# Attention with a fourth score bank, one shared output bank, and transposes four units behind the scores

## What is computed

```python
# layer 1: 16 heads of 32 channels, 512 queries and 512 context tokens, 4 batches
q = _w8a8_linear(x, wq, bq)        # 8-bit activations and weights
k = cond @ wk.T + bk
v = cond @ wv.T + bv
scores = einsum('bhnd,bhld->bhnl', q, k) / sqrt(32) + mask
attn = softmax(scores, axis=-1)
o = einsum('bhnl,bhld->bhnd', attn, v)
x = x + tanh(g) * _w8a8_linear(o, wo, bo)
# then the feed-forward of the layer, with rounded weights and activations
```

## Time and profile before

| | us | share |
|---|---|---|
| median of three runs | 1017.13 | |
| the profiled execution's own time | 1016.46 | |
| its span in the profile | 1014.7 | |
| TensorE matmuls busy | 899.2 | 89% |
| TensorE weight loads busy | 587.9 | 58% |
| VectorE busy | 673.4 | 66% |
| ScalarE busy | 573.6 | 57% |
| exponentials, line 1322, 256 of them | 175.0 | |
| masks, line 1732, 256 of them | 174.0 | |
| granted TensorE clock, mean | 0.969 of full speed | |

### The profile page before, as it was taken

One profiled execution on the slowest core, in us unless ns is written; L12 is line 12 of the kernel. 1 busy time (PEld: TensorE's weight loads), 2 busy tenths in 40 slices (PEclk: granted clock), 3 DMA queues, 4 the chain that ended last, 5 costly groups with the idle time before them and its releaser, 6 DMA issues.

```text
span 1014.7 us, 15824 instructions
## 1 busy us (share of the span) xinstructions
PE 899.2 (89%) x5592; PEld 587.9 (58%) x5592; DVE 673.4 (66%) x1870; ACT 573.6 (57%) x1094; POOL 86.9 (9%) x105
## 2 busy tenths in 40 slices
PE   3989998999999787899999999999999899999467
PEld 2868765676767453666444666445666444666233
DVE  5895860524250073798777898777798776799564
ACT  4545233355553132788347788357788447789153
POOL 2000213021120005100100000100000100000100
PEclk9999999999999999799999999999999999999769
DMA  6444556452450059510199110198110188100001
GB/s 195 141 142 159 196 205 228 146 164 86 135 198 1 23 164 197 115 43 2 42 182 191 43 43 2 42 180 186 51 43 1 43 175 196 46 2 1 1 1 42
DMA packets 52270, 102.82 MB, mean 101 GB/s; under 512 B 8924, under 2 KB 8924, under 8 KB 50656
## 3 DMA queue, kind: packets, MB, share of 16 engines
q1 hardware_dynamic: 39872, 71.88, 27.1%
q10 hardware_dynamic: 8160, 17.31, 5.1%
q0 software_dynamic: 4160, 12.62, 4.0%
HBM read 55.62 MB, written 14.75 MB: 69 GB/s over the span
## 4 chain that ended last, share of the span: by engine, by line
PE 36%; DVE 9%; issue 6%; ACT 5%; SPq 4%; DMA 3%; POOL 1%; POOLq 0%; DVEq 0%; ACTq 0%
PE psum L1494 7%; PE psum L1462 6%; PE psum L1567 5%; PE psum L1511 5%; PE psum L1537 5%; SPq L1185 4%; ACT probs L1322 3%; DMA k<-k_lo 3%; PE psum L1429 1%; PE psum L1553 1%; PE psum L1520 1%; DVE amax L1670 1%; DVE xn L1842 1%; DVE stats L1837 1%; DVE xn L1658 1%
## 5 line engine op out<-in xcount | busy, mean ns | idle before, releaser
L1322 ACT ACTIVATE probs<-psum,neg_max 128x512 f32<-128x512 f32 x256 | 175.0, 692 | 46.5 <-DVE neg_max L1732 46.5
L1732 DVE CUSTOM_DVE_ANT_0 psum<-psum,m_in 128x512 f32<-128x512 f32 x256 | 174.0, 703 | 18.3 <-issue 18.3
L1494 PE MATMUL psum<-ident,probs 128*128 128x128 f32 x1024 | 154.2, 275 | 0.0
L1494 PEld LDWEIGHTS psum<-ident,probs 128*128 128x128 f32 x1024 | 127.8, 141 | 19.8 <-issue 2.6
L1462 PE MATMUL psum<-k,q 128*128 128x512 f32 x256 | 125.7, 496 | 15.3 <-ACT probs L1322 6.8
L674 PE MATMUL psum<-w_sb,hT 128*128 128x512 f32 x256 | 117.6, 604 | 5.6 <-ACT hT L566 5.6
L1762 DVE COPY probsT<-psum 128x512 f32<-128x512 f32 x128 | 87.8, 686 | 2.7 <-PE psum L1494 2.5
L1313 ACT COPY probsT<-psum 128x512 f32<-128x512 f32 x128 | 75.3, 588 | 20.3 <-PE psum L1494 20.3
L594 PE MATMUL psum<-xselT_hi,w_hi 128*128 128x256 f32 x256 | 81.8, 320 | 1.6 <-ACT xselT_hi L501 1.6
L674 PEld LDWEIGHTS psum<-w_sb,hT 128*128 128x128 f32 x256 | 47.0, 192 | 55.3 <-issue 48.5
L1462 PEld LDWEIGHTS psum<-k,q 128*128 128x128 f32 x256 | 49.1, 192 | 51.7 <-ACT probs L1322 31.5
(11 more groups left out here) (221 smaller groups left out, 1566.7 us busy)
## 6 DMA issues: line engine op xcount, KB each, us to landing
bw_raw<-in_L_ffn_W_dram ACTq DMA_DIRECT2D x16, 1024.0 KB, 5.3
c_in<-in_ctx_dram SPq DMA_DIRECT2D x8, 1024.0 KB, 5.5
k<-k_hi SPq DMA_DIRECT2D x24, 256.0 KB, 5.9
k<-k_lo SPq DMA_DIRECT2D x24, 256.0 KB, 6.7
q<-q_hi SPq DMA_DIRECT2D x48, 128.0 KB, 3.9
q<-q_lo SPq DMA_DIRECT2D x48, 128.0 KB, 3.4
xres<-in_x_dram SPq DMA_DIRECT2D x4, 1024.0 KB, 5.9
w_raw<-in_L_ffn_w_dram POOLq DMA_DIRECT2D x4, 1024.0 KB, 5.4
```

The costliest lines, as they stand in the source:

```text
L1322: act.activation(probs[:, u % 4, :], psum[u % SCORE_BANKS][:, :], ACT.Exp, scale=-1.0, bias=neg_max[:, u:u + 1], accum_out=prob_sum[:, nt, ...
L1494: mm = pe.transpose(turn_bank(u)[:, l * P:(l + 1) * P], probs[:, u % 4, l * P:(l + 1) * P], ident[:, :])
L1732: dve.tensor_tensor_reduce(bank[:, :], bank[:, :], m_in[:, nt, :], -1.0, LOWEST, ALU.add, ALU.min, neg_max[:, u:u + 1]).then_inc(masked_re ...
```

## The change

Banks 0 to 3 hold scores, 4 to 6 turned units, and bank 7 (`OUT_BANK`) alone takes the value sum and the turned output of every half group. The transposes of a unit stand four steps behind its score, and four first scores and masks are issued ahead. The two value groups of a half group stand two steps apart. `attnT` is copied by ScalarE in the step between them (its wait spans the second group), its transposes follow three steps after the second group, and the division one step later. The first value group of a half group now waits for the division of the one just before. The context copies of ScalarE move from step 68 to step 70, which puts them behind the last `attnT` copy. The wait and the memset ahead of each mask are taken out.

```diff
-        LAG = 3
+        LAG = 4
-        SCORE_BANKS, TURN_BANKS = 3, 3
+        SCORE_BANKS, TURN_BANKS = 4, 3
-        AV_STEPS = 4
-        STEPS = UNITS + LAG + UH + 3
-        CONTEXT_BANKS = (0, 1, 2, 4)
+        AV_STEPS = 2
+        STEPS = UNITS + LAG + UH - 1
+        OUT_BANK = 7
+        CONTEXT_BANKS = (0, 1, 2, 3)
...
# ScalarE
-                        if more and s == UNITS + LAG + 1:
+                        if more and s == UNITS + LAG + 2:
                             turned_context(b + 1)
...
-                        hg = past_half_group(s, 1)
+                        hg = past_half_group(s, -6)
                         if hg is not None:
                             act.wait_ge(av_psum, b * HG + hg + 1)
-                            act.copy(attnT[:, hg % 2, :], psum[6 + hg % 2][:, 0:HALF]).then_inc(av_ready, 1)
+                            act.copy(attnT[:, hg % 2, :], psum[OUT_BANK][:, 0:HALF]).then_inc(av_ready, 1)
...
# TensorE
+                            elif b and SCORE_BANKS + u == OUT_BANK - 1:
+                                pe.wait_ge(x_done, b * T)
...
-                        if 0 <= hg < HG and i % AV_STEPS == 0:
+                        if 0 <= hg < HG and i in (0, AV_STEPS):
...
-                                if hg >= 2:
-                                    pe.wait_ge(o_ready, b * HG + hg - 1)
+                                if hg:
+                                    pe.wait_ge(o_ready, b * HG + hg)
                                 else:
                                     pe.wait_ge(x_done, b * T + 1)
-                            for l in range(T * i // UH, T * (i + AV_STEPS) // UH):
+                            for l in range(T * i // (2 * AV_STEPS), T * (i + AV_STEPS) // (2 * AV_STEPS)):
...
-                        hg = past_half_group(s, 3)
+                        hg = past_half_group(s, -2)
                         if hg is not None:
                             pe.wait_ge(av_ready, b * HG + hg + 1)
...
# VectorE
-                    if u >= 4:
-                        dve.wait_ge(probs_ready, b * UNITS + u - 3)
-                    dve.memset(held[:, u % 4:u % 4 + 1], 0.0)
...
-                        hg = past_half_group(s, 2)
+                        hg = past_half_group(s, -2)
...
-                        hg = past_half_group(s, 3)
+                        hg = past_half_group(s, -1)
```

More of the change, by code:

```diff
@@ L1503, in attend @@
                                     context(b + 1, c_in)
-                                if hg >= 2:
-                                    pe.wait_ge(o_ready, b * HG + hg - 1)
+                                if hg:
+                                    pe.wait_ge(o_ready, b * HG + hg)
                                 else:
                                     pe.wait_ge(x_done, b * T + 1)
-                            for l in range(T * i // UH, T * (i + AV_STEPS) // UH):
+                            for l in range(T * i // (2 * AV_STEPS), T * (i + AV_STEPS) // (2 * AV_STEPS)):
                                 for r in range(HPG):
                                     h = (hg // 2) * HPG + r
-                                    mm = pe.matmul(psum[6 + hg % 2][HD * r:HD * (r + 1), 0:HALF],
+                                    mm = pe.matmul(psum[OUT_BANK][HD * r:HD * (r + 1), 0:HALF],
                                                    vv[:, l, h * HD:(h + 1) * HD],
@@ L1519, in attend @@
                             for k in range(2):
-                                mm = pe.transpose(psum[6 + hg % 2][:, HALF + k * P:HALF + (k + 1) * P],
+                                mm = pe.transpose(psum[OUT_BANK][:, HALF + k * P:HALF + (k + 1) * P],
                                                   attnT[:, hg % 2, k * P:(k + 1) * P], ident[:, :])
@@ L1777, in attend @@
                                 xn[:, n0:n0 + 2, g * P:(g + 1) * P].rearrange("p t (r d) -> p t r d", r=HPG),
-                                psum[6 + hg % 2][:, HALF:2 * HALF].rearrange("p (t r d) -> p t r d", t=2, r=HPG),
+                                psum[OUT_BANK][:, HALF:2 * HALF].rearrange("p (t r d) -> p t r d", t=2, r=HPG),
                                 prob_inv[:, n0:n0 + 2, g * HPG:(g + 1) * HPG].unsqueeze(3).broadcast_to([P, 2, HPG, HD]),
```

## The result

The changed kernel took 1030.0 us (median of 4, 1029.44 to 1031.15) against 1017.21 us before (median of 4, 1016.01 to 1017.87). The ratio is 1.0134, 95% interval 1.0114 to 1.0154; the medians lie 12.8 us apart, slower. The profiled executions, on which all that follows rests, were 1029.44 and 1016.46 us, with spans of 1027.7 and 1014.7: +13.0. The forecast was +8.6, so the sign and the range held and the size was a third short.

A forecast was written before the change was run, and what follows sets the result against it. The prediction took a loop between TensorE and ScalarE, period 8.75 us, as the bound, no engine alone. Periods +4.6, starts +0.75 and ends +3.25 gave +8.6 on 1016.46, so 1025.0 us, range 1019 to 1031.

The forecast's parts named there:

- The steady loop: Attention's repeating half group: a chain over the wait at `attnT` lengthens the period from 8.75 to 8.94, +0.19, 24 times.
- No phase shift between engines gets round a chain that returns to itself: Attention loop: the chain from value group over `attnT` and eight ScalarE instructions to the next value group cannot be avoided.
- The single output bank: First value group's added wait for the previous half group's division: hidden by the loop, cost nothing.
- The bank rule cited in the forecast: Skill rule for independent matmul groups to rotate through PSUM banks; by it copy, transposes and division would show in full.
- The memset: Memsets ahead of each mask on VectorE, 256 at 59 ns, 15.1 us in all: removing them taken as zero.
- The start: Start of attention in batches 1 to 3: fourth early score ahead of the down product, +0.25 each, bounds 0 and 0.50.
- The end: End of a batch: context copies behind `attnT` delay the next keys, +1.25 in three batches; last batch saves 0.5.
- a gap of over 1 us on TensorE ahead of the keys: Sign at a batch's end that would show the forecast right, together with context copies after the last `attnT`.
- The upper side of the range: Range up to 1031, taking in the slower rival with late masks or division; the forecast alone reaches 1029.
- A: Faster rival: scores stop waiting for exponentials, period about 8.07, time about 1004; chance 0.12.
- B: Rival at batch ends: keys start later but slack absorbs it, 1021.3; chance 0.08.
- C: Slower rival: VectorE late on the loop's last masks, or the division late, 0.2 us more per period, 1029.8; chance 0.10.

The follow-up runs named there:

- k: Changed kernel, value groups still two steps apart, with `attnT` copied two steps later and output transposes at -1: ratio 1.0091 to the kernel before, period 9.18 us.
- a: Kernel before with its value groups two steps apart instead of four, nothing else changed: period 9.12 us instead of 8.75.
- g: Kernel before with the four residual preparations spread over steps 19, 27, 35 and 43: ratio 0.9906 to the kernel before.
- e: Changed kernel with the four residual preparations of a batch spread, one in each of four half groups: 1019.35 us.
- f: Changed kernel with value groups four steps apart, `attnT` and output transposes moved to fit, and residual preparations spread: 1000.98 us, ratio 0.9831 to the kernel before.
- c: Changed kernel with the wait and the memset ahead of each mask put back: 1031.1 us against 1030.0.
- i: Kernel before without the wait and the memset ahead of each mask: ratio 0.9993 to the kernel before.
- h: Kernel before with four score banks and two banks for turned units: ratio 1.0035 to the kernel before.
- b: Changed kernel with ScalarE's context copies put back ahead of the last `attnT` copy (step 68): ratio 1.0050 to the kernel before.
- d: Changed kernel with value groups four steps apart again, `attnT` four steps behind the first group, output transposes at six: 1006.99 us.

## Why the prediction was right in sign and short in size

**The steady loop: right number, half of the reason.** Period, second group and `attnT` came out within 0.01 us. But I named one chain, over the wait at `attnT`, and there are two of almost the same length. The second goes from the first group over the second group (2.54), the transposes behind it (452.48) and the copy that needs them (453.22, so 4.62 after the first group) to the next first group (4.33 later). In the changed kernel the chain over `attnT` comes last, by very little: ScalarE idles ahead of `attnT` and not ahead of the copy at 453.22. Run k, where that copy really waits, has it 4.56 after the group, so the second chain alone would give about 4.56 + 4.33 = 8.89, still more than 8.75. Run k takes the wait at `attnT` away and the second chain remains, longer by the `attnT` copy that now stands inside it (4.56 + 4.62 = 9.18). Run a has no wait at `attnT` either: 4.75 + 4.37 = 9.12, with the output transposes behind the second group. So both chains run over the second group, and what costs is that it stands so close behind the first. The sentence that put the +0.19 down to a wait put "inside the two groups" is right for this order and incomplete: an edit made by it, moving the copy alone, lengthens the period to 9.18 (k).

The forecast also took all six stretches between half groups 0 and 6 for plain periods of 8.75, 52.5 us, where the kernel before had 54.17. The rest is the residual's clump (run g: 52.52). That did no harm to the difference, since the changed kernel pays nearly the same for it (55.20 less the 53.70 of run e).

**"No phase shift between engines gets round a chain that returns to itself"** was right for this order and hid the point: with four steps between the groups and the other parts of the change the loop falls to 8.47. Something among these other parts is then worth 0.28 a period against the kernel before; that this is the fourth bank or the lag is not shown.

**The single output bank "cost nothing": half wrong.** True in plain periods. In the residual's half group it is a wait of 2.27 us. At full clock this makes the stretch no longer than before: two periods around it take 19.40 in batch 2 (743.68 to 763.08), 1.5 over two plain ones, and 19.11 before (734.27 to 753.38), 1.6 over two plain ones. VectorE's clump cost that much in either kernel. But before, TensorE had no gap of that size ahead of a value group (9.7 us over the whole kernel, none of it behind a division); now it has one per batch, and the low clock follows it in two batches of four. The bank rule cited in the forecast, that groups should rotate through banks, is not what decides here: in plain periods the division is done 0.66 us before the bank is wanted again, and with one bank run f is the fastest of all the kernels here. No run has the order of f with two output banks, so what rotation would add to it is open.

**The memset: right,** shown in both directions (c and i), up to the 0.12 us a batch of run c.

**The start: right,** 0.16 a batch for a forecast of 0.25, within its bounds of 0 and 0.50: the down product is 0.23 longer with the fourth early score in it, and the first value group follows it 0.07 sooner.

**The end: right in kind, 0.99 for 1.25.** I had put the second value group 1.00 behind the first; as one run of 32 they took 1.93 together, and the first of them stood at 9.24 and not 9.33, so `attnT` came 11.24 after the reference and not 11.46.

**What was missing: the low clock, +7.8.** Every term of the sum took TensorE's durations as given. The forecast even named "a gap of over 1 us on TensorE ahead of the keys" as a sign to look for, and did not price what stands behind such a gap: sixteen products that took 8.83 instead of 7.03. Run b takes the gap away, and with it the slow keys, though the low clock of the up projection grew in the same run. Run e takes the wait of the residual's half group away, and with it the low clock there. Runs c and e also show how much of this is chance: c has the wait at the residual and no low clock behind it, e has the gap ahead of the keys and no low clock behind it. The Trainium skill, TensorE: Matmul & The Clock Gate, section HAM oscillation, describes a loop that falls back to the low clock behind a wait at every tile; here it followed some of the gaps and not others (keys 8.83 and 7.13 behind the same 1.52 us).

That the measured time lies inside the forecast's range is in part luck. The upper side of the range was kept for late masks and for what the durations might do, and what filled it was the low clock, for which it had no term. Two more parts of the +13.0, the 1.0 us of low clock at the up projection and the 1.4 us by which batch 0 started earlier, are not shown to come of the change at all and happen to cancel.

**The rivals.** A (1004) did not come: the chain decided, as forecast. The rule beside it (the Trainium skill, Perfetto Trace Analysis, section Optimization Strategy, where it stands and not in the section that the forecast names: repeating gaps can mean too few buffers) did not give the outcome here: with the fourth bank the gaps of the earlier trace rows left the scores (15.3 to 6.6 us), those ahead of the value products grew (9.7 to 32.5), and the time rose. It is not refuted as such. Run h gives up a turn bank for the score bank, and in runs d and f, which have the fourth bank, the period is shorter than before. B (1021.3) is out: keys came later and nothing absorbed it. C (1029.8) has nearly the measured time and not its mechanism: masks are not late in plain periods, and its "division late" holds in one half group of eight. A right total by C would have been luck.

**Open.** Why a 1.52 us gap ahead of the keys is followed by low clock in batches 0 and 2 and not in batch 1 or in e (7.13, granted clock 1.00), and what decides it at the residual. The runs of one kernel spread with it (k: 1020.48 to 1031.87 us, mean granted clock 0.972 and 0.964). Not tried: three score and two output banks with the order of d, which would tell what the fourth bank and the lag are worth; and four score banks and three turn banks with the groups close but the second one placed behind the transposes that ScalarE needs next.

## What to carry to other kernels

In a loop over several in-order engines, write down every chain that returns to its start, not the first that explains the number; two chains of nearly equal length look like one, and taking one away shows the other. The place of a large block (here 16 value products, 1.0 us) in an engine's list decides which small result behind it is late: keep such blocks apart, and spread clumps of side work over the periods before adding buffers. Where an edit opens gaps on TensorE like those here (1.5 and 2.3 us), add a term for the clock behind each, from nothing to what was seen here, 1.6 to 1.8 us. And before a faster stretch is put down to an edit, look where else in the trace the low clock has gone.

## What the hardware showed that was not expected

The low clock reaches well past its gap: keys 8.83 for 7.03 us behind 1.52 us of idle time, and 3.52 for 2.54 us between two value groups behind 2.27 us. It does not follow each time, and when it stays away in one place it can come in another: run b saved 3.7 us of slow keys and lost 2.9 us more in its up projections. The context copies moved two steps in one engine's list came with 8.4 us, of which the traces put 5.0 down to the wait that the move removed.
